# Row maxima of attention: turned by VectorE in 32x32 blocks and regrouped over a DRAM buffer, in place of TensorE transposes copied out by ScalarE

## What is computed

```python
scores = jax.nn.softmax(jnp.einsum('bhse,bhte->bhst', q, k) * scale, axis=-1)
att = jnp.einsum('bhst,bhte->bhse', scores, v)
```

## Time and profile before

| | |
|---|---|
| median of 3 runs | 2131.88 us (2129.2 to 2137.05) |
| the profiled execution: time, span | 2135.92 us, 2134.1 us |
| TensorE matmuls busy | 86% |
| VectorE, ScalarE, GpSimd busy | 75%, 67%, 20% |
| mean granted TensorE clock | 0.934 |
| moved by DMA | 140.87 MB |

### The profile page before, as it was taken

One profiled execution on the slowest core, in us unless ns is written; L12 is line 12 of the kernel. 1 busy time (PEld: TensorE's weight loads), 2 busy tenths in 40 slices (PEclk: granted clock), 3 DMA queues, 4 the chain that ended last, 5 costly groups with the idle time before them and its releaser, 6 DMA issues.

```text
span 2134.1 us, 38850 instructions
## 1 busy us (share of the span) xinstructions
PE 1831.3 (86%) x10958; PEld 688.9 (32%) x10958; DVE 1598.7 (75%) x3593; ACT 1432.2 (67%) x2921; POOL 432.8 (20%) x570
## 2 busy tenths in 40 slices
PE   4858989888988988888898888989898998998775
PEld 1232323333332333333333333323333332333322
DVE  4538888887878778778787878777787878888471
ACT  2716686776767677677766767676776768776543
POOL 2112131221212122121212212120121213121200
PEclk9957999999999999999999999999999999999867
DMA  5203223050413205041320504123050413212020
GB/s 109 71 11 101 47 67 96 18 140 17 118 34 96 65 17 140 17 115 37 81 81 17 140 17 115 36 71 91 17 140 17 115 37 79 79 35 59 29 53 16
DMA packets 162647, 140.87 MB, mean 66 GB/s; under 512 B 38761, under 2 KB 144050, under 8 KB 162482
## 3 DMA queue, kind: packets, MB, share of 16 engines
q1 hardware_dynamic: 162482, 139.29, 24.7%
HBM read 77.38 MB, written 55.57 MB: 62 GB/s over the span
## 4 chain that ended last, share of the span: by engine, by line
PE 37%; issue 24%; DMA 11%; ACT 9%; POOL 8%; DVE 8%; SPq 3%; ACTq 0%; POOLq 0%; DVEq 0%
PE ps L1127 11%; PE ps L1112 7%; PE ps L1148 5%; ACT probs L647 5%; DVE neg_max L853 4%; PE ps L1102 4%; DMA k_stack<-k_rows 4%; DMA rden_all<-rden_rows 3%; PE ps L1078 3%; PE ps L1153 2%; PE ps L1191 2%; DMA k_rows<-kp 2%; PE ps L1141 2%; POOL o_raw L551 2%; POOL qk L561 2%
## 5 line engine op out<-in xcount | busy, mean ns | idle before, releaser
L853 DVE TENSOR_REDUCE neg_max<-ps 128x1 f32<-128x512 f32 x2048 | 1316.4, 680 | 196.8 <-PE ps L1102 167.7
L647 ACT ACTIVATE probs<-ps 128x512 f32<-128x512 f32 x2048 | 1093.4, 599 | 324.5 <-PE ps L1112 309.0
L1102 PE MATMUL ps<-k_stack,q_stack 48*128 48x512 bf16 x2048 | 702.5, 402 | 86.6 <-DVE neg_max L853 46.4
L1112 PE MATMUL ps<-q_stack,k_stack 50*128 50x512 bf16 x2048 | 655.1, 391 | 79.8 <-ACT probs L647 75.7
L1127 PE MATMUL ps<-probs,v_aug 128*32 128x512 f32 x4096 | 568.1, 628 | 1.0
L1112 PEld LDWEIGHTS ps<-q_stack,k_stack 50*128 50x128 bf16 x2048 | 150.8, 95 | 525.1 <-ACT probs L647 342.4
L1102 PEld LDWEIGHTS ps<-k_stack,q_stack 48*128 48x128 bf16 x2048 | 159.3, 94 | 280.3 <-DVE neg_max L853 239.4
L551 POOL TENSOR_TENSOR o_raw<-o_raw,rden_all 128x512 f32<-128x512 f32 x64 | 81.3, 1270 | 569.6 <-DMA rden_all<-rden_rows 569.6
L1127 PEld LDWEIGHTS ps<-probs,v_aug 128*32 128x32 f32 x4096 | 81.7, 109 | 136.3 <-issue 81.5
L1153 PE MATMUL ps<-wo,o_raw 128*128 128x128 f32 x512 | 81.8, 326 | 43.2 <-POOL o_raw L551 43.1
L653 ACT ACTIVATE xn<-x,shift,rstd 128x128 f32<-128x128 f32 x192 | 80.5, 484 | 52.4 <-POOL shift L534 52.4
(11 more groups left out here) (103 smaller groups left out, 1499.4 us busy)
## 6 DMA issues: line engine op xcount, KB each, us to landing
q_stack<-q_rows SPq DMA_DIRECT2D x128, 192.0 KB, 3.7
k_stack<-k_rows SPq DMA_DIRECT2D x128, 192.0 KB, 4.6
rden_all<-rden_rows SPq DMA_DIRECT2D x64, 256.0 KB
q_rows<-qp SPq DMA_DIRECT2D x32, 384.0 KB, 2.6
k_rows<-kp SPq DMA_DIRECT2D x32, 384.0 KB, 2.9
q_rows<-qp SPq DMA_DIRECT2D x32, 256.0 KB, 3.0
k_rows<-kp SPq DMA_DIRECT2D x32, 256.0 KB, 3.0
x_in<-in_L_attn_x SPq DMA_DIRECT2D x16, 256.0 KB, 2.8
```

What stands on the lines that cost most here:

```text
L647: act.activation(probs[:, u % RING, :], ps[:, bank_of(l, u), :], ACT.Exp).then_inc(exps, 1)
L853: dve.tensor_reduce(neg_max[l][:, pair // 2, col:col + 1], ps[:, BANKS + bank_of(l, n), :], AX.X, ALU.max, negate=True).then_inc(max_taken, 1)
L1102: pe.matmul(ps[:, BANKS + bank_of(l, m), :], q_stack[l][row:row + KROWS, pair, tok:tok + 128], k_stack[l][row:row + KROWS, pair, :], start ...
L1112: pe.matmul(ps[:, bank_of(l, u), :], k_stack[l][row:row + AROWS, pair, tok:tok + 128], q_stack[l][row:row + AROWS, pair, :], start=True, s ...
```

## The change

The eight `m` pieces of TensorE and ScalarE's `take_max` are gone. VectorE writes both bfloat16 parts into one tile (`m_parts`, 128 x 32 per quarter) and, one half step after `parts_low`, transposes each 32x32 block of it in place of its partition block (`parts_turn`, to `m_turned`). SP's `max_rows` now has three DMAs per quarter in place of two: `m_turned` (128 partitions of 64 bytes, 8 KB) to the DRAM buffer `m_rows`, a wait until that has landed (`m_out`), and two DMAs from `m_rows` into `q_stack`, each of 64 runs of 64 bytes, which put the four token blocks side by side. The places of `max_rows` in SP's order are the same.

```diff
-            def take_max(l, quarter, b):
-                act.wait_ge(written[f"m{l}"], 4 * b + quarter + 1)
...
-                copy(m_parts[l][quarter % 2][:, :], gen[0:32, 0:128]).then_inc(read[f"m{l}"], 1)
...
-                elif name[0] == "m":
-                    l, quarter = int(name[1]), int(name[2])
-                    pe.wait_ge(low_done[l], 4 * b + quarter + 1)
-                    last = turn(gen[0:32, 0:128], neg_max[l][:, quarter, :])
...
+        m_rows = [nc.dram_tensor(f"m_rows{l}", (4, 128, 32), BF16).ap() for l in (0, 1)]
...
-                hold(read[f"m{l}"], 4 * b + quarter + 1)
+                hold(turn_done[l], 4 * b + quarter + 1)
+                sp.dma_start(m_rows[l][quarter], m_turned[l][:, quarter, :]).then_inc(m_out[l], 16)
+                hold(m_out[l], 16 * (4 * b + quarter + 1))
                 for e in (0, 1):
                     sp.dma_start(q_stack[l][HALF * e + KROWS:HALF * e + AROWS, 2 * quarter:2 * quarter + 2, :],
-                                 m_parts[l][quarter % 2][16 * e:16 * e + 16, :]).then_inc(m_in[l][quarter], 16)
+                                 bass.AP(m_rows[l].tensor, (128 * quarter + 16 * e) * 32,
+                                         [[8 * 32, MROWS], [32, 8], [32 * 32, 4], [1, 32]])
+                                 ).then_inc(m_in[l][quarter], 16)
...
+            def parts_turn(l, quarter, b):
+
+                dve.wait_ge(low_done, 4 * maxima_before(l, b) + quarter + 1)
+                need(dve, m_in[l][quarter], 32 * b)
+                dve.transpose(m_turned[l][:, quarter, :], m_parts[l][:, quarter, :]).then_inc(turn_done[l], 1)
...
                         if work in have and e == 0 and step % 8 == 0 and 0 < step <= STEPS:
                             parts_low(l, step // 8 - 1, b)
+                        if work in have and e == 1 and step % 8 == 0 and 0 < step <= STEPS:
+                            parts_turn(l, step // 8 - 1, b)
```

More of the change, by code:

```diff
@@ L38 @@
 BANKS = 3
[L41 to L45, removed]
+X_PE = ((1, "xt0"), (3, "q0"), (5, "k0"), (7, "qt"), (8, "kt"), (11, "pr1"), (14, "v1"),
+        (19, "xt3"), (21, "rt"), (27, "ct"), (29, "out"))
+Y_PE = ((7, "v0"), (9, "pr0"), (13, "xt1"), (14, "g0"), (15, "u0"), (16, "g1"),
+        (17, "u1"), (18, "g2"), (19, "u2"), (21, "dn"), (25, "xt2"), (26, "qka"), (27, "qkb"),
+        )
 PIECE = {"qt": (-1, "M2"), "kt": (-1, "M2"), "v1": (-1, "M2"),
@@ L66, in sem_name @@
 def sem_name(piece):
-    return piece[0:2] if piece[0] == "m" else piece
+    return piece
 def count(piece, b):
-    return 4 * b + int(piece[2]) + 1 if piece[0] == "m" else b + 1
+    return b + 1
 def parts_of(kind, i):
@@ L213, in build @@
         v_aug = [sb(f"v_aug{l}", [128, TT, HEADS, 32]) for l in (0, 1)]
-        neg_max = [sb(f"neg_max{l}", [128, 4, 32]) for l in (0, 1)]
-        neg_high = [sb(f"neg_high{l}", [128, 4, 16], BF16) for l in (0, 1)]
-        m_parts = [[sb(f"m_parts{l}{k}", [32, 128], BF16) for k in (0, 1)] for l in (0, 1)]
+        neg_max = [sb(f"neg_max{l}", [128, 4, 16]) for l in (0, 1)]
+        m_parts = [sb(f"m_parts{l}", [128, 4, 32], BF16) for l in (0, 1)]
+        m_turned = [sb(f"m_turned{l}", [128, 4, 32], BF16) for l in (0, 1)]
         probs = sb("probs", [128, RING, SEQ])
@@ L294, in build @@
         high_done = sem("high_done")
-        low_done = [sem(f"low_done{l}") for l in (0, 1)]
+        low_done = sem("low_done")
+        m_out = [sem(f"m_out{l}") for l in (0, 1)]
+        turn_done = [sem(f"turn_done{l}") for l in (0, 1)]
         m_in = [[sem(f"m_in{l}{q}") for q in range(4)] for l in (0, 1)]
@@ L729, in slot @@
                     apply_norm(0, x_in, range(TT), 1)
-                    take_max(0, 0, 0)
                     return
@@ L740, in slot @@
                         exp_unit(0 if kind == "X" else 1, 2 * s + 1, i if kind == "X" else i - 1)
-                    for at_step, name in slot_pieces(kind, at):
-                        if at_step == s and name[0] == "m":
-                            take_max(int(name[1]), int(name[2]), i + PIECE[name][0])
                     if kind == "X":
@@ L851, in max_tile, with split_max @@
                 pair, st, e = n // 8, (n // 2) % 4, 1 - n % 2
-                col = 16 * e + 4 * (pair % 2) + st
+                col = 8 * e + 4 * (pair % 2) + st
                 dve.tensor_reduce(neg_max[l][:, pair // 2, col:col + 1], ps[:, BANKS + bank_of(l, n), :], AX.X,
                                   ALU.max, negate=True).then_inc(max_taken, 1)
+            def split_max(l, quarter, part):
+                return m_parts[l][:, quarter, :].rearrange("p (e j c) -> p e j c", e=2, j=2)[:, :, part, :]
             def parts_high(l, quarter, b):
                 dve.wait_ge(max_taken, 2 * STEPS * maxima_before(l, b) + 16 * (quarter + 1))
-                dve.tensor_copy(neg_high[l][:, quarter, :].rearrange("p (e c) -> p e c", e=2),
-                                neg_max[l][:, quarter, :].rearrange("p (e j c) -> p e j c", e=2, j=2)[:, :, 0, :]
+                dve.tensor_copy(split_max(l, quarter, 0), neg_max[l][:, quarter, :].rearrange("p (e c) -> p e c", e=2)
                                 ).then_inc(high_done, 1)
@@ L865, in parts_low @@
                 dve.wait_ge(high_done, 4 * maxima_before(l, b) + quarter + 1)
-                parts = neg_max[l][:, quarter, :].rearrange("p (e j c) -> p e j c", e=2, j=2)
-                high = neg_high[l][:, quarter, :].rearrange("p (e c) -> p e c", e=2)
-                dve.tensor_tensor(parts[:, :, 1, :], parts[:, :, 0, :], high, ALU.subtract).then_inc(low_done[l], 1)
+                dve.tensor_tensor(split_max(l, quarter, 1), neg_max[l][:, quarter, :].rearrange("p (e c) -> p e c", e=2),
+                                  split_max(l, quarter, 0), ALU.subtract).then_inc(low_done, 1)
+            def parts_turn(l, quarter, b):
+                dve.wait_ge(low_done, 4 * maxima_before(l, b) + quarter + 1)
+                need(dve, m_in[l][quarter], 32 * b)
+                dve.transpose(m_turned[l][:, quarter, :], m_parts[l][:, quarter, :]).then_inc(turn_done[l], 1)
             def take_v(l, s, b):
```

## The result

The changed kernel takes 2230.43 us (median of 4 runs, 2226.43 to 2235.3) against 2132.68 us of the kernel before in the same comparison: a ratio of 1.0458, 95% interval 1.0426 to 1.0491. It is 98 us slower. The forecast was 2177 us and a range up to 2226; the direction was right, the size half of what came, and the time lies just above the range.

A forecast was written before the change was run, and what follows sets the result against it. No engine was full (TensorE 86% busy); TensorE waited for SP's DMA chain in X, and VectorE set the pace ahead of Y's projection. Terms 22 + 28 + 7 + 5 + 4 - 21 = +45 us gave 2177 us, range 2116 to 2226.

The forecast's parts named there:

- A: X slot, quarter 2: the store's round trip issues the layer 1 stacks 1.6 us later, 14 times: +22 us.
- B: X slot, quarter 3: store queues behind the DMA backlog, new 2.0 us wait at half step 48, 14 times: +28 us.
- C: Y slot: quarter 1's round trip makes the denominators leave 0.45 us later, 15 times: +7 us.
- D: VectorE: 128 added transpositions, costing time only in three of eight places per period where it is full: +5 us.
- F: TensorE and ScalarE: removed transposes and copies gain at four of eight places, 1.39 us per period, 15 times: -21 us.
- clock rival: New waits at half steps 32 and 48 leave TensorE at the lower clock: up to 23 us more, 2200 us; chance 0.12.
- E: First and last slots: nothing runs beside the maxima, first quarter waited for in full, twice about 2 us: +4 us.

The follow-up runs named there:

- filler run: Changed kernel with nine extra matmuls, results unused, on TensorE in front of its wait at half step 32: 2231.02 us, ratio 1.0463.

## Why the prediction was right and wrong

**A, quarter 2, mis-sized.** The chain was right to a tenth: the stacks start 1.5 us later (1.6 foretold), half step 32 waits about 2 us (2.5 foretold). The step that failed is "TensorE would have waited for `k_stack` six half steps later anyway, so that is no second loss". The wait at half step 32 is one that the lower clock follows, in 10 of 12 periods at half step 36, where the kernel before had none; the step from half step 32 to 36 takes 0.45 us longer, and in 7 of the 12 periods TensorE then comes too late to wait for `k_stack` at all. The place costs 2.4 us (X 28 to X 40), not 1.6; the run with quarter 2 on the old way removed it. In the changed kernel as it is, the 0.8 us more do not add to the period: half step 48 waits for SP's chain, and the filler run, which had won 1.06 us by half step 40, lost all of it there.

**B, quarter 3, mis-sized.** Store behind the backlog, loads behind the store, wait at half step 48: all as foretold, and shown by moving the traffic. SP waited 3.6 to 6.2 us in the loop, 5.1 on average, against 4.7 foretold. With A and `m03` I had the period 1.6 + 2.0 - 0.4 = 3.2 us longer behind half step 48; from X 28 to X 60 it grows by 4.3. Of the 1.1 us more, 0.6 lie up to X 48: 0.4 are the store's longer wait, and from the first load's issue to half step 48 it is 2.7 to 2.9 us where the sum has 2.5. The other 0.4 come between X 48 and X 60, where the lower clock shows in 4 of 12 periods at half step 52 and before in none.

**C, Y slot.** The denominators' chain grew by 0.3 us up to Y 20 (0.45 foretold). But between Y 20 and Y 28 another 1.0 us is lost, which I had nowhere; there the lower clock is granted at half step 28 in 9 of 12 periods, before in 4. With both quarters on the old way this shrinks to 0.3 us and 5 of 12. Whether the longer wait for the projection or the shifted course of the whole period brings it wasn't tried.

**D, VectorE,** 202 ns per transposition against 183 taken, 25.8 us of busy time: nothing of it can be seen in the stretches where VectorE is full (Y 0 to Y 16 grows by 0.1 us).

**F, the gain, failed.** 21 us were credited for TensorE and ScalarE at four places; the run that kept their work beside the new way was 6 us slower. `m03` now lies ahead of the new wait at half step 48: what TensorE gains there it waits longer, as B had it. `m10`, `m12` and `m13`, 0.95 us per period, show nothing: `m13` is gone, and from Y 32 to the next X 0 the difference stays at 5.4 us; `m10` is gone too in the run with both quarters on the old way, and from X 48 to X 60 it gains nothing (-0.08 to -0.02). The step that failed is "Of the eight per period I count the four where TensorE sets the pace": I had read an idle TensorE in front of the transpose as a sign of that. That the tiles behind it are paced by the other engines fits these rows but was not tested by itself.

**The clock rival** had the right mechanism, and its evidence against (full clock behind a wait of 1.72 us) came from a single row: in the kernel before the granted clock at half step 40, just behind this wait, is at the lower level in 4 of the loop's 12 periods. It was to be part of the forecast, since A and B make such waits.

**The sum.** Per loop period I had 1.6 + 2.0 + 0.45 + 0.3 - 1.4 = 3.0 us; measured are 5.37. Of the 2.4 missing, 1.1 are in the X slot (A and B), 1.0 between Y 20 and Y 28, 0.95 the gain that didn't come, less 0.35 that C and D had too much and 0.3 gained up to X 28. What lies outside the loop cost 27 us, where three periods and E had come to 13; X slot 1 alone took 8. The range was narrower than its own terms: 7 to 29 for A, up to 42, 16, 23 and 8 for the others and -21 for F are +97 us or 2229 us with every upper bound added, so "without adding up every bound" does not hold for the 2230 us; the upper end was put at 2226, and F, the term that failed, was held fixed in it.

## What to carry to other kernels

A round trip over DRAM is priced at the place where its store joins the traffic: the same 8 KB took 1.5 us at six places of the period, 2.15 at one (quarter 2) and 5 at one (quarter 3), and from another engine's queue no less. Where a change puts a new wait ahead of an old one, ask what TensorE's clock does after it before calling it covered; and a gain for an engine is lost at the next wait for a chain that doesn't contain it. Taking a wait out of a queue also lets out what stood behind it, as quarter 3 on GpSimd's queue showed. When a chain of DMAs is what is waited for, shorten that: one wait split in two in the kernel before was worth 1.3%.

## What the runs showed of the hardware

A store of 128 runs of 64 bytes to DRAM, issued by SP, took 1.4 us from issue to landing as its median, and up to 6.4 us behind large transfers. Issued by GpSimd, it was back after 5.2 to 6.1 us in the loop and after 2.56 us in X slot 15, without the large transfers. The Trainium skill, "DMA: Bandwidth & Descriptors", section "Anatomy of one DMA", has a fixed cost of about 2.0 us for a DMA that GpSimd issues; SP's quiet stores are below that.

A 128x32 bfloat16 transposition on VectorE took 202 ns, 194 to 212. The lower TensorE clock of 0.50 was granted during or just behind idle waits of about 2 us at half step 32, for 10.2 us in the period shown. With nine tenths of such a wait filled by matmuls of no use it stayed at 1.00 in 9 of 12 periods at half step 36, against 2 of 12 without them.
